# Attention rewritten: layer 0's two attentions in one phase, 256-query jobs, row offsets from four side-by-side products, one maximum over four heads

## The chip, the core and the metric

The kernel runs on one core of a Trainium2 chip. The metric is the device time of one execution in microseconds (us). The engines are TensorE (PE in the profile, its weight loads PEld), VectorE (DVE), ScalarE (ACT), GpSimd (POOL) and SyncE (SP, which here only issues DMAs; SPq is its queue). Each engine runs its own list of instructions in order, and they wait for each other through semaphores.

## What is computed

Two layers, each of an attention block and a mixture of experts, on x of 2 x 1024 tokens, 512 wide, with a context of 2 x 2048 tokens, 256 wide. Only the attention blocks are touched:

```python
# layer 0, 16 heads of 32, on the layer-normed x
att = einsum('bhqd,bhkd->bhqk', q, k) * scale          # 1024 queries x 1024 keys
y = einsum(softmax(where(causal, att, -inf)), v)       # "self", causal
attc = einsum('bhqd,bhkd->bhqk', qc, kc) * scale       # 1024 queries x 2048 keys
y = y + einsum(softmax(attc), vc)                      # "cross"
x = x + tanh(g_xattn[0]) * (y @ Wp + bp)
# layer 1: one cross attention of the same size
x = x + tanh(g_xattn[1]) * (softmax(q1 k1^T * scale) v1 @ Wo + bo)
```

The experts between and behind them, the routing and the projections are the same in both kernels.

## The kernel before

The program is a row of phases: proj0, projc, self0, cross0, out0, route0, ffn0, proj1, attn1, out1, route1, ffn1. A barrier of all engines stands between two phases. A phase of attention works off eight units (2 batches x 4 groups of four heads of 32). The names in the profile are those of the tiles, with digits left out: self_, cross_ and attn_ are the three phases of attention.

A unit is a `Job` with two sides. One is the **scores side**: in steps of 128 keys x 512 queries, PE makes the scores of each of four heads (L692, keys as weights, queries moving), ACT takes their exponentials out of PSUM into `probs` (L789), and PE multiplies these with the values (`pv`) and with ones (`den`), four heads side by side on 32 columns of the array each (L745). About half of the steps leave their sum with ones to POOL, which adds the exponentials up in `psums` (L657), so that `den` takes one product for all of them. A cross unit has 32 such steps, a self unit 12, of which the causal ones are narrower and take a mask product (L696). The other is the **maximum side**: the softmax needs a number to subtract for each query, and it rides in the score product itself. Queries and keys are stored as three stacked blocks of 32 rows (high part, high or low part, low part, so that fp32r products come out exact), and row 96 of the queries holds minus the row's maximum against a row of ones in the keys. These maxima come from a second full score product, with queries as weights and keys moving (L676, mask L680), which VectorE reduces one bank of 512 at a time (L812), or two at a time before the first unit (L823). After the last of a unit, VectorE takes the maximum over the parts, PE transposes it (L721), VectorE negates it (L839), and SP writes it into row 96 by four DMAs (L610).

While one unit's scores side runs, the next unit's maximum side is laid between its products: `timetable` writes one order of events for a pair of units from costs per column, and every engine follows it. The first unit's maxima have nothing to be laid beside: they run alone before the first step of the phase ("group" events), after the loads. Scores go through three banks of PSUM (`BANKS = 3`), and so do the maxima. VectorE inverts the denominators, 512 per partition (L851), and multiplies (L854).

SP loads each unit by eight DMAs (three of keys L586, three of queries L590, two of values L595), three units at the start of a phase, later ones as one of three sets of buffers comes free. The events that the last steps below lean on:

```python
pe.wait_ge(exped, i * (GH * per["steps"]) + (item + 1))   # scores: a bank is free
...
for b in bufs:
    load(next(w for w, j in enumerate(jobs) if j.buf == b), 0, 0)   # SP, at the start
```

## Time and profile before

| | us |
|---|---|
| median of three runs | 4876.4 (4874.72 to 4880.6) |
| span of the profiled execution | 4872.1 |
| self0: first score to the last product of numerator and inverse | 496 to 963 |
| cross0: the same | 1075 to 2056 |
| attn1: the same | 2887 to 3870 |
| PE busy | 4298.1 (88%) |
| VectorE, ScalarE, GpSimd busy | 2731.9, 1960.3, 1360.6 |
| mean granted TensorE clock | 0.903 |

The span is 4.3 us below the median of the runs, and there is nothing of the program outside it. Busy time of PE is the union of its records; a product's record is longer than the distance to the next one, so the distance between starts is what a product costs in a stream. In a view in order of time, a row with a count merges neighbours of one form: its first number is the start of the first, its second the time to the end of the last.

### The profile page before, as it was taken

What the parts mean: (1) busy time and instruction counts of PE and PEld (TensorE: products, weight loads), DVE (VectorE), ACT (ScalarE), POOL (GpSimd) and SP (SyncE); (2) the same over time, 40 slices, a digit from 0 to 9 for tenths busy, and PEclk for the clock granted to TensorE, in tenths of its full rate; (3) what the DMA queues carried; (4) which work ended last, traced back from release to release, by engine and by line L of the source; (5) the groups of instructions that cost most, each with busy time, mean ns of one, the idle gap of its engine ahead of it and who ended that gap; (6) DMA issues with size and microseconds to landing.
All of it is one profiled execution on the core that took longest, in us unless ns stands there. A gap on an engine that the chain in (4) does not pass through costs nothing. (4 is left out here: it accounts for less than half of the span.)

```text
span 4872.1 us, 69058 instructions
## 1 busy us (share of the span) xinstructions
PE 4298.1 (88%) x22146; PEld 2564.5 (53%) x22146; DVE 2731.9 (56%) x4193; ACT 1960.3 (40%) x3433; POOL 1360.6 (28%) x619
## 2 busy tenths in 40 slices
PE   7897999879999999772999489999999763999998
PEld 5776555434444444242998344444444243888886
DVE  4354555367777777147665377767776156434432
ACT  2121333315555555501665215555555401434432
POOL 0000111215555555500111215555555400101111
PEclk9997778859999999975999769999999975999999
DMA  5488233061221220142664552221210032334331
GB/s 170 157 294 246 44 71 70 25 131 23 50 50 41 50 53 5 35 150 77 206 208 151 153 107 47 50 50 42 50 33 5 33 121 97 110 112 122 117 114 37
DMA packets 260270, 451.21 MB, mean 93 GB/s; under 512 B 19216, under 2 KB 102160, under 8 KB 253840
## 3 DMA queue, kind: packets, MB, share of 16 engines
q1 hardware_dynamic: 245904, 409.83, 29.4%
q0 software_dynamic: 14080, 37.76, 3.3%
...
q14 instruction: 130, 1.06, 0.1%
...
## 5 line engine op out<-in xcount | busy, mean ns | idle before, releaser
L657 POOL TENSOR_TENSOR attn_psums<-attn_psums,attn_probs 128x1024 f32<-128x1024 f32 x224 | 531.5, 2396 | 527.4 <-PE attn_pv L745 295.2
L657 POOL TENSOR_TENSOR cross_psums<-cross_psums,cross_probs 128x1024 f32<-128x1024 f32 x224 | 531.4, 2396 | 526.4 <-PE cross_pv L745 294.5
L812 DVE TENSOR_REDUCE attn_partscross<-attn_banks 128x1 f32<-128x512 f32 x896 | 560.1, 683 | 145.9 <-PE attn_banks L676 140.1
L789 ACT ACTIVATE attn_probs<-attn_banks 128x512 f32<-128x512 f32 x960 | 497.9, 604 | 357.6 <-PE attn_banks L692 343.2
L789 ACT ACTIVATE cross_probs<-cross_banks 128x512 f32<-128x512 f32 x960 | 497.8, 604 | 357.3 <-PE cross_banks L692 343.2
L812 DVE TENSOR_REDUCE cross_partscross<-cross_banks 128x1 f32<-128x512 f32 x896 | 560.0, 683 | 145.2 <-PE cross_banks L676 139.8
L676 PE MATMUL cross_banks<-cross_keys,cross_queries 96*128 96x512 f32 x1024 | 408.8, 461 | 37.9 <-DMA cross_values<-l_cross_values 37.9
L676 PE MATMUL attn_banks<-attn_keysy,attn_queriesy 96*128 96x512 f32 x1024 | 408.8, 461 | 37.3 <-DMA attn_valuesy<-l_cross_values 37.3
L1444 DVE TENSOR_TENSOR ffn_wL<-ffn_raw,ffn_wH 128x2048 fp32r<-128x2048 f32 x128 | 293.4, 2293 | 222.6 <-ACT ffn_wH L1399 222.6
L692 PE MATMUL attn_banks<-attn_queriesy,attn_keysy 97*128 97x512 f32 x1024 | 375.3, 425 | 31.1 <-ACT attn_probs L789 19.9
L692 PE MATMUL cross_banks<-cross_queries,cross_keys 97*128 97x512 f32 x1024 | 375.6, 425 | 29.8 <-ACT cross_probs L789 19.7
L1399 ACT ACTIVATE ffn_wH<-ffn_raw 128x2048 fp32r<-128x2048 f32 x128 | 245.2, 1916 | 358.1 <-DMA ffn_raw<-in_L_ffn_W_dram 197.2
L1356 PE MATMUL ffn_up<-ffn_xH,ffn_wH 128*128 128x256 f32 (+1 forms) x1024 | 350.7, 342 | 2.7 <-DVE ffn_xL L1450 2.7
L676 PEld LDWEIGHTS cross_banks<-cross_keys,cross_queries 96*128 96x128 f32 x1024 | 187.9, 204 | 305.9 <-DVE cross_partscross L812 205.4
L676 PEld LDWEIGHTS attn_banks<-attn_keysy,attn_queriesy 96*128 96x128 f32 x1024 | 187.9, 204 | 305.5 <-DVE attn_partscross L812 205.4
L1356 PE MATMUL ffn_up<-ffn_xH,ffn_wL 128*128 128x256 f32 (+1 forms) x1024 | 347.1, 339 | 0.0
L1356 PE MATMUL ffn_up<-ffn_xL,ffn_wH 128*128 128x256 f32 (+1 forms) x1024 | 347.0, 339 | 0.0
L1371 PE MATMUL ffn_down<-ffn_wH,ffn_hH 128*128 128x512 f32 x768 | 306.7, 399 | 0.0
L1371 PE MATMUL ffn_down<-ffn_wH,ffn_hL 128*128 128x512 f32 x768 | 304.5, 396 | 0.0
L1371 PE MATMUL ffn_down<-ffn_wL,ffn_hH 128*128 128x512 f32 x768 | 304.3, 396 | 0.0
L692 PEld LDWEIGHTS attn_banks<-attn_queriesy,attn_keysy 97*128 97x128 f32 x1024 | 187.3, 190 | 209.9 <-ACT attn_probs L789 143.9
L692 PEld LDWEIGHTS cross_banks<-cross_queries,cross_keys 97*128 97x128 f32 x1024 | 187.5, 190 | 209.1 <-ACT cross_probs L789 142.3
...
## 6 DMA issues: line engine op xcount, KB each, us to landing
ffn_raw<-in_L_ffn_W_dram SPq DMA_DIRECT2D x128, 1024.0 KB, 5.4
...
```

Of the source, the lines that this page charges most:

```text
L657: pool.tensor_tensor(psums[:, heads, :], psums[:, heads, :], probs[:, (n["steps"] + s) % RING, heads, :], ALU.add).then_inc(pooled_sum, 1)
L676: mm = pe.matmul(out[:, 0:cols], QS[a.buf][0:3 * HD, h, qt * P:(qt + 1) * P], KS[a.buf][0:3 * HD, h, part * BLK:part * BLK + cols], start= ...
L692: mm = pe.matmul(out[:, n0:], KS[b.buf][0:3 * HD + 1, h, kb * P:(kb + 1) * P], QS[b.buf][0:3 * HD + 1, h, qb * BLK + n0:(qb + 1) * BLK], s ...
L789: act.activation(out[:, h, n0:], sc[:, item % BANKS, n0:], ACT.Exp, scale=SCALE).then_inc(exped, 1)
L812: dve.tensor_reduce(parts[a.kind][:, h * (T // P) + qt, part:part + 1], mx[:, item % BANKS, 0:cols], AX.X, ALU.max).then_inc(max_read, 1)
L1356: mm = pe.matmul(up[ft % UP][:, 0:k], w[:, cols], x[:, ch, :], start=n == 0, stop=n == 3 * C - 1)
L1371: mm = pe.matmul(down[st][:, :], h[:, ft, st * P:(st + 1) * P], w[:, cols], start=ft == 0 and n == 0, stop=ft == FT - 1 and n == 2)
L1399: act.activation(wH[:, m % RING, :], raw[:, m % RING, :], ACT.Copy).then_inc(high_made, 1)
L1444: dve.tensor_tensor(wL[:, m % RING, :], raw[:, m % RING, :], wH[:, m % RING, :].bitcast(F32), ALU.subtract).then_inc(low_made, 1)
```

## The change

`Job` and `timetable` go, and `Unit`, a new `Job` and `Plan` come. A unit is now cut into four jobs of 256 queries, a job into steps of two blocks of 128 keys; a step makes four items of two heads x 256 queries, one bank of PSUM and one exponential each. A cross unit has again 32 steps, a self unit 10. Layer 0's sixteen units (eight self, eight cross) are one phase `attn0` without a barrier between. Nothing is a hardware loop any more.

- The row offset no longer comes from the exact product. The high parts of queries and keys are loaded once more in a flat layout (`QN`, `KN`: head h on partitions 32h to 32h+31), and a group is four products of 32 rows, one per head, into four banks (`mx`, one set for all groups), then four masks where the diagonal is met. VectorE reduces the four banks by one instruction over 4 x 512. PE waits for that before the next group. A job's maxima are due four steps before its first step; 8 groups come before step 0, then mostly one a step in cross units, two in six of the ten steps of a self unit.
- The turned maxima go through a scores bank and are negated by ScalarE; SP writes them by two DMAs per job.
- Numerator and denominator share one bank `acc`; ScalarE takes both out at a job's end. The denominators go by DMA into a layout of 8 per partition, are inverted, go to DRAM and come back spread over 32 partitions; POOL multiplies.
- Two sets of unit buffers in place of three. SP loads unit 0; unit 1 and all later ones are loaded by ScalarE's queue: two flat DMAs right after the unit two back has had its last group, eight stacked ones right after that unit's last step.

The core of the diff:

```diff
+QB = 256
+STEP = 2
+LEAD = 4
...
+class Job:
...
+        if unit.causal:
+            d = 2 * qb
+            self.blocks = [(kb, 0, False) for kb in range(d)] + [(d, 0, True), (d + 1, P, True)]
+        else:
+            self.blocks = [(kb, 0, False) for kb in range(unit.keys // P)]
+        self.steps = len(self.blocks) // STEP
+        self.last = first + self.steps - 1
+        self.groups = []
+        for t in range(QB // P):
+            n = (qb * (QB // P) + t + 1) * P if unit.causal else unit.keys
+            self.parts = -(-n // BLK)
+            for part in range(self.parts):
+                cols = min(BLK, n - part * BLK)
+                self.groups.append((t, part, cols, unit.causal and part == self.parts - 1))
+        whole = [kb for kb, n0, masked in self.blocks if not masked]
+        inner = [kb for kb in whole if kb < len(self.blocks) - 3]
+        self.pooled = [kb for kb in inner if kb < 2 or kb % 2 == 0] if len(inner) > 2 else []
...
+class Plan:
...
+        due = [self.jobs[j].first - LEAD for j, _ in self.groups]
+        done = 0
+        while done < len(due) and due[done] <= 0:
+            self.groups_at[-1].append(done)
+            done += 1
+        for m in range(n):
+            need, k = 0, 0
+            for g in range(done, len(due)):
+                k += 1
+                if due[g] - m > 24:
+                    break
+                need = max(need, -(-k // (due[g] - m + 1)))
+            now = self.jobs[self.job_of[m]]
+            for _ in range(max(need, 1)):
+                if done == len(due):
+                    break
+                j = self.groups[done][0]
+                if j > self.job_of[m] + 3 or self.jobs[j].u > now.u + 1:
+                    break
+                self.groups_at[m].append(done)
+                done += 1
...
+            self.turn_at[m + 2 if m >= 0 and m + 2 < n else -1 if m < 0 else m].append(j)
...
-def attention(nc, name, c, jobs, body, repeats, sources, yT, ring=2):
+def attention(nc, name, c, units):
...
+    RING, SC, DEEP, BUFS = 3, 3, 4, 2
+        KS = [ph.sb(f"keys{b}", [P, GH, KEYS], F32R) for b in range(BUFS)]
+        KN = [ph.sb(f"keysn{b}", [P, KEYS], F32R) for b in range(BUFS)]
+        QN = [ph.sb(f"queriesn{b}", [P, T], F32R) for b in range(BUFS)]
+        sc = ph.ps("sc", (P, SC, BLK))
+        mx = ph.ps("mx", (P, GH, BLK))
+        acc = ph.ps("acc", (P, 2, QB))
...
+        def load_flat(eng, u):
+            unit, b = units[u], u % BUFS
+            eng.dma_start(KN[b][:, 0:unit.keys].bitcast(F32), unit.k_src[unit.row, :, 0, :]).then_inc(flat_in[b], DMA)
+            eng.dma_start(QN[b][:, :].bitcast(F32), unit.q_src[unit.row, :, 0, :]).then_inc(flat_in[b], DMA)
+        def load_stack(eng, u):
+            unit, b = units[u], u % BUFS
+            for row, half in ((0, 0), (1, 1), (2, 0)):
+                eng.dma_start(KS[b][row * HD:(row + 1) * HD, :, 0:unit.keys].bitcast(F32),
+                              unit.k_src[unit.row, :, half, :].rearrange("(h d) n -> d h n", d=HD)
+                              ).then_inc(stack_in[b], DMA)
+            for row, half in ((0, 0), (1, 0), (2, 1)):
+                eng.dma_start(QS[b][row * HD:(row + 1) * HD, :, :].bitcast(F32),
+                              unit.q_src[unit.row, :, half, :].rearrange("(h d) n -> d h n", d=HD)
+                              ).then_inc(stack_in[b], DMA)
...
+                load_flat(sp, 0)
+                load_stack(sp, 0)
+                for j in plan.turn_at[-1]:
+                    set_row(j)
+                for m in range(N_STEPS + 8):
+                    for back, move in ((2, take_den), (3, put_inv), (4, take_over), (7, store)):
+                        if 0 <= m - back < N_STEPS and plan.ends(m - back) is not None:
+                            move(plan.ends(m - back))
+                    for j in plan.turn_at.get(m, ()):
+                        set_row(j)
...
+                def maxima(k):
+                    j, g = plan.groups[k]
+                    job, (t, part, cols, masked) = jobs[j], jobs[j].groups[g]
+                    b = job.u % BUFS
+                    if job.qb == 0 and g == 0:
+                        pe.wait_ge(flat_in[b], FLAT * DMA * (job.u // BUFS + 1))
+                    if k:
+                        pe.wait_ge(max_read, k)
+                    q0 = (job.qb * (QB // P) + t) * P
+                    for h in range(GH):
+                        rows_h = slice(h * HD, (h + 1) * HD)
+                        mm = pe.matmul(mx[:, h, 0:cols], QN[b][rows_h, q0:q0 + P],
+                                       KN[b][rows_h, part * BLK:part * BLK + cols], start=True, stop=True)
+                    if masked:
+                        for h in range(GH):
+                            mm = pe.matmul(mx[:, h, cols - P:cols], c["identr"][:, :], c["maskq"][:, :],
+                                           start=False, stop=True, skip_group_check=True)
+                    mm.then_inc(max_ready, 1)
...
+                def scores(m, i):
+                    j, item = plan.job_of[m], plan.item[m, i]
+                    job = jobs[j]
+                    b = job.u % BUFS
+                    if m == job.first and i == 0:
+                        if job.qb == 0:
+                            pe.wait_ge(stack_in[b], STACK * DMA * (job.u // BUFS + 1))
+                        pe.wait_ge(row_set[j % DEEP], ROW * DMA * (j // DEEP + 1))
+                    if item >= SC:
+                        pe.wait_ge(exped, item - SC + 1)
+                    kb, n0, masked = job.blocks[(m - job.first) * STEP + i // 2]
+                    for half in range(2):
+                        h = 2 * (i % 2) + half
+                        out = sc[:, item % SC, half * QB:(half + 1) * QB]
+                        mm = pe.matmul(out[:, n0:], KS[b][0:3 * HD + 1, h, kb * P:(kb + 1) * P],
+                                       QS[b][0:3 * HD + 1, h, job.qb * QB + n0:(job.qb + 1) * QB], start=True, stop=True)
+                        if masked:
+                            mm = pe.matmul(out[:, n0:n0 + P], c["identr"][:, :], c["maskk"][:, :],
+                                           start=False, stop=True, skip_group_check=True)
+                    mm.then_inc(scored, 1)
...
+                pe.wait_ge(ones_set, BUFS)
+                for k in plan.groups_at[-1]:
+                    maxima(k)
+                for j in plan.turn_at[-1]:
+                    turn(j)
+                for m in range(N_STEPS + 1):
+                    if m < N_STEPS:
+                        for i in range(3):
+                            scores(m, i)
+                        for k in plan.groups_at[m]:
+                            maxima(k)
+                    if m:
+                        values(m - 1)
+                    if m < N_STEPS:
+                        for j in plan.turn_at[m]:
+                            turn(j)
+                        scores(m, 3)
...
+                load_flat(act, 1)
+                load_stack(act, 1)
+                for j in plan.turn_at[-1]:
+                    turned(j)
+                for m in range(N_STEPS + 1):
+                    if m < N_STEPS:
+                        for i in range(3):
+                            exponent(m, i)
+                    if m and plan.ends(m - 1) is not None:
+                        drain(plan.ends(m - 1))
+                    if m < N_STEPS:
+                        for j in plan.turn_at[m]:
+                            turned(j)
+                        exponent(m, 3)
+                    for u in range(len(units) - BUFS):
+                        if m == max(plan.unit_max_at[u], 0) + 1:
+                            act.wait_ge(max_ready, plan.unit_groups[u])
+                            load_flat(act, u + BUFS)
+                        if m == plan.last_of[u] + 1:
+                            act.wait_ge(valued, plan.last_of[u] + 1)
+                            load_stack(act, u + BUFS)
...
+                def reduce(k):
+                    j, g = plan.groups[k]
+                    t, part, cols, _ = jobs[j].groups[g]
+                    dve.wait_ge(max_ready, k + 1)
+                    dve.tensor_reduce(parts[j % DEEP][:, :, t, part], mx[:, :, 0:cols], AX.X, ALU.max
+                                      ).then_inc(max_read, 1)
+                    if g == len(jobs[j].groups) - 1:
+                        dve.wait_ge(max_read, k + 1)
+                        if j >= 2:
+                            dve.wait_ge(exped, plan.turn_item[j - 2] + 1)
+                        dve.tensor_reduce(top[:, j % 2, :].rearrange("p (t h) -> p h t", h=GH),
+                                          parts[j % DEEP][:, :, :, 0:jobs[j].parts], AX.X, ALU.max
+                                          ).then_inc(top_ready, 1)
...
-        for kind, keys_n, own, y in (("self", T, (queries, keys, values), y_self),
-                                     ("cross", TC, (cross_queries, cross_keys, cross_values), y_cross)):
-            jobs = [Job(kind, f"{u % 3}", keys_n, kind == "self") for u in range(UNITS)]
-            attention(nc, f"{kind}0", c, jobs, 3, 2, {kind: own}, y)
+        attention(nc, "attn0", c,
+                  [Unit(T, True, queries, keys, values, y_self, u) for u in range(UNITS)] +
+                  [Unit(TC, False, cross_queries, cross_keys, cross_values, y_cross, u) for u in range(UNITS)])
...
-        jobs = [Job("cross", f"y{u % 3}", TC, False) for u in range(UNITS)]
-        attention(nc, "attn1", c, jobs, 3, 2, {"cross": (l1_queries, l1_keys, l1_values)}, y1)
+        attention(nc, "attn1", c, [Unit(TC, False, l1_queries, l1_keys, l1_values, y1, u) for u in range(UNITS)])
```

The order of PE in the middle of a cross unit, before (cross_banks are scores and maxima, L692 the scores and L676 the maximum products, pv and den values and sums):

```order
L676 MATMUL cross_banks<-cross_keys,cross_queries 128x512 [waits cross0_max_read] x2
L692 MATMUL cross_banks<-cross_queries,cross_keys 128x512 [waits cross0_exped]
L676 MATMUL cross_banks<-cross_keys,cross_queries 128x512 [waits cross0_max_read]
L692 MATMUL cross_banks<-cross_queries,cross_keys 128x512 [waits cross0_exped] x2
L676 MATMUL cross_banks<-cross_keys,cross_queries 128x512 [waits cross0_max_read]
L692 MATMUL cross_banks<-cross_queries,cross_keys 128x512 [waits cross0_exped]
L745 MATMUL cross_pv<-cross_probs,cross_values 32x512 [waits cross0_exped]
L745 MATMUL cross_pv<-cross_probs,cross_values 32x512 x3
L676 MATMUL cross_banks<-cross_keys,cross_queries 128x512 [waits cross0_max_read] x3
L745 MATMUL cross_den<-cross_probs,keep_onesf 32x512 x4
```

One step of a cross unit on PE now, from the last item of the step before on (attn_sc are scores, attn_mx the group of the maximum, attn_acc values and sums):

```order
L682 MATMUL attn_sc<-attn_queries,attn_keys 128x256 [waits attn0_exped]
L682 MATMUL attn_sc<-attn_queries,attn_keys 128x256
L682 MATMUL attn_sc<-attn_queries,attn_keys 128x256 [waits attn0_exped]
L682 MATMUL attn_sc<-attn_queries,attn_keys 128x256
L682 MATMUL attn_sc<-attn_queries,attn_keys 128x256 [waits attn0_exped]
L682 MATMUL attn_sc<-attn_queries,attn_keys 128x256
L682 MATMUL attn_sc<-attn_queries,attn_keys 128x256 [waits attn0_exped]
L682 MATMUL attn_sc<-attn_queries,attn_keys 128x256
L653 MATMUL attn_mx<-attn_keysn,attn_queriesn 128x512 [waits attn0_max_read]
L653 MATMUL attn_mx<-attn_keysn,attn_queriesn 128x512 x3
L699 MATMUL attn_acc<-attn_probs,attn_values 32x256 [waits attn0_exped]
L699 MATMUL attn_acc<-attn_probs,attn_values 32x256 x7
```

Four maximum products scattered among the scores have become one group between the third item's scores and the values, and the first item in the piece is the one whose exponential the fourth item of the piece waits for.

ScalarE at the change of a cross unit now (attn_both is the taking out of numerator and denominator); before, these DMAs stood on SP and ScalarE had none:

```order
L758 ACTIVATE attn_probs<-attn_sc 128x512 [waits attn0_scored] x2
L767 ACTIVATE attn_both<-attn_acc 128x512 [waits attn0_normed,attn0_job_done]
L758 ACTIVATE attn_probs<-attn_sc 128x512 [waits attn0_scored]
L541 DMA attn_keys<-l_cross_keys 32x4x2048 [waits attn0_valued]
L541 DMA attn_keys<-l_cross_keys 32x4x2048 x2
L545 DMA attn_queries<-l_cross_queries 32x4x1024 x3
L550 DMA attn_values<-l_cross_values 128x8x128 x2
L758 ACTIVATE attn_probs<-attn_sc 128x512 [waits attn0_scored,attn0_added,attn0_valued]
```

Eight DMAs now stand between two exponentials.

## Rows read from the trace of the kernel before

**Rows 1.** Busy time by stage, first score to last output (columns: stretch, length, busy by engine with count, granted clock, DMA share, GB/s)
```profile
496.00:963.00 467.00, 451.41 (x2615) 251.50 (x2615) 247.83 (x398) 174.07 (x401) 79.15 (x32) 0.80 0.22 49
1075.00:2056.00 981.00, 950.85 (x5127) 400.58 (x5127) 645.23 (x958) 537.93 (x1040) 531.45 (x224) 0.99 0.16 34
2887.00:3870.00 983.00, 950.71 (x5127) 400.59 (x5127) 645.70 (x958) 539.19 (x1041) 531.46 (x224) 0.99 0.16 34
```

**Rows 2.** PE in order of time, middle of cross0 (start, length, engine, line, tiles, count)
```profile
1501.79 0.40 PE L676 MATMUL cross_banks<-cross_keys,cross_queries 96*128 96x512 f32 x1
1502.03 0.42 PE L692 MATMUL cross_banks<-cross_queries,cross_keys 97*128 97x512 f32 x1
1502.38 1.06 PE L745 MATMUL cross_pv<-cross_probs,cross_values 128*32 128x512 f32 x8
1503.37 0.96 PE L676 MATMUL cross_banks<-cross_keys,cross_queries 96*128 96x512 f32 x3
```

**Rows 3.** Groups by line, shapes kept apart, cross0 (count, busy us, mean ns, idle before)
```profile
L812 DVE TENSOR_REDUCE cross_partscross<-cross_banks 128x1 f32<-128x512 f32 x896 | 560.0, 683 | 145.2 <-PE cross_banks L676 139.8 <-issue 3.6 <-DVE cross_y L854 0.2
L823 DVE TENSOR_REDUCE cross_partscross<-cross_banks 128x2 f32<-128x1024 f32 x64 | 72.5, 1210 | 34.2 <-PE cross_banks L676 34.2
L789 ACT ACTIVATE cross_probs<-cross_banks 128x512 f32<-128x512 f32 x960 | 497.8, 604 | 357.3 <-PE cross_banks L692 343.2 <-POOL cross_psums L657 11.4 <-issue 2.7
L657 POOL TENSOR_TENSOR cross_psums<-cross_psums,cross_probs 128x1024 f32<-128x1024 f32 x224 | 531.4, 2396 | 526.4 <-PE cross_pv L745 294.5 <-ACT cross_probs L789 231.9
```

**Rows 4.** PE in order of time, ffn0: fp32r products of 256 columns
```profile
2402.03 0.28 PE L1356 MATMUL ffn_up<-ffn_xL,ffn_wH 128*128 128x256 f32 x1
2402.15 0.28 PE L1356 MATMUL ffn_up<-ffn_xH,ffn_wL 128*128 128x256 f32 x1
```

**Rows 5.** PE in order of time, self0: 256- and 128-column groups of four heads
```profile
801.22 0.61 PE L745 MATMUL self_den<-self_probs,keep_onesf 128*32 128x256 f32 x8
801.65 1.04 PE L745 MATMUL self_den<-self_psums,keep_onesf 128*32 128x512 f32 x8
...
802.73 0.40 PE L745 MATMUL self_den<-self_probs,keep_onesf 128*32 128x128 f32 x8
803.06 0.50 PE L692 MATMUL self_banks<-self_queries,self_keys 97*128 97x512 f32 x1
803.40 0.22 PE L696 MATMUL self_banks<-keep_maskk,keep_identr 128*128 128x128 f32 x1
```

**Rows 6.** PE in order of time, cross0 after a unit's last maximum
```profile
1188.67 0.94 PE L692 MATMUL cross_banks<-cross_queries,cross_keys 97*128 97x512 f32 x3
1189.84 0.50 PE L692 MATMUL cross_banks<-cross_queries,cross_keys 97*128 97x512 f32 x1 [0.23 <-ACT cross_probs L789]
```

**Rows 7.** SP's queue in order of time: one unit's load, self0 and cross0
```profile
566.77 1.57 SPq L586 DMA_DIRECT2D self_keys<-l_keys  x3
568.43 1.60 SPq L590 DMA_DIRECT2D self_queries<-l_queries  x3
570.22 1.32 SPq L595 DMA_DIRECT2D self_values<-l_values  x2
...
1206.56 1.59 SPq L586 DMA_DIRECT2D cross_keys<-l_cross_keys  x3
1209.99 16.15 SPq L595 DMA_DIRECT2D cross_values<-l_cross_values  x2
```

**Rows 8.** Order of time, all engines: how the three phases begin
```profile
438.75 1.50 SPq L586 DMA_DIRECT2D self_keys<-l_keys  x3
...
962.25 0.69 DVE L854 TENSOR_TENSOR self_y<-self_numer,self_denom 128x512 f32<-128x512 f32 x1
...
1074.78 2.76 PE L692 MATMUL cross_banks<-cross_queries,cross_keys 97*128 97x512 f32 x5 [4.30 <-DMA cross_queries<-cross_topT]
...
2779.43 1.30 SPq L586 DMA_DIRECT2D attn_keysy<-l_cross_keys  x3
...
2887.32 2.27 PE L692 MATMUL attn_banks<-attn_queriesy,attn_keysy 97*128 97x512 f32 x4 [4.36 <-DMA attn_queriesy<-attn_topT]
```

**Rows 9.** Busy time and DMA rate while attn1's first loads run
```profile
2781.00:2802.00 21.00, 0.00 (x0) 0.00 (x0) 0.00 (x0) 0.00 (x0) 18.94 (x3) 0.50 1.01 207
```

602 lines of the change are left out of this document (214 added, 388 removed).

## The prediction

> **What bounds the kernel now.** I read the busy time by stage first. In the two cross stages PE is busy 951 of 981 and 983 us at a granted clock of 0.99, while VectorE has 645, ScalarE 400 to 540 and POOL 531; self0 has PE at 451 of 467 but the clock at 0.80 [rows 1]. So PE's stream is the bound, and I cost it by distances between starts: a 512-column product of scores or maxima 0.24 (1501.79 to 1502.03), one block of values over four heads 0.99 with leaving the column mode, and 0.35 in place of 0.24 before it, so 0.11 for going in [rows 2]; 256 columns 0.12 [rows 4]; four heads of 256 columns 0.43, of 128 columns 0.33 with 0.11 of leaving, and the first product after them 0.34, so 0.10 of weight load that nothing hides [rows 5]. Per cross step of before that gives scores 4 x 0.236 = 0.94, maxima the same, values 0.86, sums 9/16 x 0.86 = 0.48, and 1.56 visits to the column mode x 0.3 = 0.47: 3.70, against 981/256 = 3.83 measured. The account misses 3 to 4% of small waits; I carry that on.
>
> **Part 1, a cross step (512 of them).** The maxima shrink from four exact products to one group. No row of before shows four products of 32 rows side by side. If they run like the column groups, a group costs one product, 0.24, plus 0.10 for its weights and 0.09 for the change of mode: 0.43. If they run one by one, it costs 0.94 + 0.1 = 1.04. I take the lower end less a little of the weight load, 0.41, since the nearest rows are the column groups: four heads leave eight records there, which one by one at 0.24 would need 1.9 and take 0.88 [rows 2], so they do lie side by side.
> The gain is not the whole 0.6, because of the scores' ring. There are three banks as before, but the order is now fixed: item 3 of a step, items 0, 1 of the next, and item 2 waits until item 3's exponential is out. The trace shows that chain by itself: three scores from 1188.67, the next at 1189.84, released by ScalarE, 1.17 later [rows 6], where three items need only 0.72. Two products of 256 end together as one of 512 does (0.12 + 0.28 is near 0.42 to 0.50 [rows 2, 4, 6]). So a step is: chain 1.17, item 2 with exposed weights 0.34, group 0.41, into the column mode 0.09, values 2 x 0.44 = 0.88, sums 18/16 x 0.43 = 0.48, out 0.11: 3.48. The turns of the maxima add 0.06, unmodelled waits 0.05: **3.6**. A phase's eight units give 256 x 3.6 = 922, plus 10 for the last job's denominators (three DMA hops, of which one shows as 4.3 [rows 8]): 932 against 981 and 983. **-100** for both.
> What hides the rest: VectorE's reduce of 4 x 512. Its slope is (1210 - 683)/512 = 1.03 ns a column [rows 3], so 683 + 3 x 512 x 1.03 = 2265 ns; with the group ahead of it and the semaphores its cycle is 2.84 of 3.6, and PE's wait for the previous reduce costs nothing. That cover is 0.75 us; below a step of 2.85 VectorE would set the pace. ScalarE has 4 x 0.60, POOL seven sums of 2.4 per eight steps [rows 3]: neither binds. ScalarE's taking out of a job's bank, one more instruction of about 0.6 per eight steps, and the row writes, 4.3 us a hop [rows 8] against a lead of four steps (14 us), I cost at nothing: next late would be PE's first values of a job, a step behind the taking out.
>
> **Part 2, the loads on ScalarE.** Before, SP issues a unit's eight DMAs and nobody waits for SP. A cross unit's take it from 1206.56 to 1226.14, 19.6 us, of which 16.15 are the two of values, against 4.8 us for a self unit (566.77 to 571.54) [rows 7]. SP is thus held until much of what is queued has moved. Now the same eight stand in ScalarE's queue between two exponentials. PE can run on until it needs an exponential, about 1.4 us; then it stands. I take 19.6 - 1.4 + 2 (PE comes back at the granted 0.50 that an idle PE has [rows 9]; estimate) = 20 us. Fourteen stack loads are of cross size (units 8 to 15 of attn0, six in attn1): **+280**. The two bounds of the price: 16.15 is a queue's hold that ScalarE may not have, then 5 us as for self (14 x 17.5 = 245 less); at the rate of 207 GB/s [rows 9] the stack's 5.8 MB take 28 us, if the issue were held to the end: 14 x 8 = 112 more. The row of the very same eight transfers is nearest. The flat loads, two DMAs of about 0.5 each, hide under PE's lead. The Trainium skill's page "DMA: Bandwidth & Descriptors", section "Issuing engines are not separate DMA queues", says that the sequencer time of initiating is usually small relative to the transfer; by that rule these +280 would be about +35, and the row of 16.15 us speaks against it here.
>
> **Part 3, the self stage.** Before, 467/8 = 58.4 per unit [rows 1]. Now a unit has 10 steps of 20 blocks and 12 groups. PE's work: scores and masks 13.1 (10.5 at full clock, divided by the 0.80 of the stage), groups 12 x 0.41 = 4.9, their masks 3.5, values 16 x 0.43 + 4 x 0.22 = 7.8, sums 5.6, changes of mode 2.0: 36.9. Waits: the ring 10 x 0.4 = 4.0; the second group of a step waits for the reduce of the first, six times, 0.68 + 1.74 + 4 x 2.26 + 6 x 0.23 = 12.9; turns 0.8; the self-size stack load 4.8 - 1.6 = 3.2. That is 57.8; two more because the clock, at 0.80 with PE nearly full, will hardly rise with PE two thirds full: 60, **+14** over eight units. Here the saved products are paid back as waits for one set of `mx`.
>
> **Part 4, ends of phases.** The barrier and the cold start of cross0 go: from 962.25 + 0.69 to 1074.78 [rows 8]: **-112**. That stretch held loads and the first unit's maxima alone; the maxima of unit 8 now fall into the last self unit's free steps, its loads are in flight a unit earlier. The starts that stay: attn0 loads two units at once, 9.4 MB at 207 GB/s [rows 9] = 46 us from 438.75 [rows 8], first score at 486 against 496: **-10**. attn1: 14.7 MB, 71 us from 2779.43, first score 2852 against 2887.32 [rows 8]: **-36**; its eight groups (26 us) hide under the rest of that load.
>
> **Sum:** -100 + 280 + 14 - 112 - 10 - 36 = +36 on 4872.1. The profiled span lies 4.3 below the median of the runs: 4876.4 + 36 = 4912; I say 4910.
>
> **The rivals.**
> *A, the queue does not hold ScalarE.* Its ring has no other traffic, while SP's carried row writes and outputs; then a stack load costs 4 to 5 us of issue as self's does: 4910 - 245 = 4665, faster than before. For it: six of the eight issues are short even in the cross row. Against: the two long ones are the last, which looks like a full queue and not like SP. It decides from about 17 us a load downwards: under 20 - 36/14 = 17.4 the sum is below zero.
> *B, the four products do not run side by side.* Then a group costs 0.60 more: 512 x 0.60 = 307, about 5215. The change would not do what it says. Against it: column groups do run so [rows 2, 5]. The Trainium skill ("TensorE: Matmul & The Clock Gate", Part 3) has four row tiles of 32 with N = 512 measured at 3.07 times one by one; 0.94/3.07 = 0.31 would be the group, 0.1 under mine; that lowers B's chance, and no row here bears on it.
> *C, the ring does not bite.* If item 3's exponential comes sooner than the case of [rows 6] tells, where ScalarE may have been behind, the step is 3.2: 512 x 0.4 = 205 less, 4705. Against: 1.17 is product, 0.60 exponential and semaphores, all still there.
> *D, the self stage gets a worse clock.* PE busy 37 of 60 may hold the granted clock nearer to the 0.50 of an idle PE [rows 9] than to 0.80; 36.9 x (0.80/0.62 - 1) = 10 per unit: +80, 4990. For it: the clock is at 0.80 already with more work [rows 1].
>
> **How the numbers follow.** Forecast 0.43 (own range 4800 to 5010: the step +-0.1 gives +-50, the load +-3 us gives +-42, the self stage +-20), A 0.16, B 0.09, C 0.14, D 0.18. About +-0.2%, 10 us, is what a measurement of this kernel can tell from no change. Faster: A, C and a fifth of the forecast's case, 0.39; same: a sixth of that case, 0.07; slower: its rest, B and D, 0.54. The range holds 8 in 10 from 4640 (just under A) to 5130 (D or the forecast with the longer hold; most of B, and A with C, lie outside).
>
> **What would show it.** On ScalarE at each change of a cross unit a stretch of some 16 to 20 us without an exponential, PE idle beside it, 14 times; cross steps at 3.6 with item 2's first product idle about 0.4 behind ScalarE, once a step; a group's four products starting within 0.1 of each other (B: 0.24 apart); VectorE's reduce near 2.26 us; the second group of a self step waiting for VectorE; self units near 60 and the granted clock there 0.75 to 0.80 (D: under 0.7); first scores near 486 and, in attn1, some 71 us behind its first load. The forecast is wrong above all if a load holds ScalarE for much less or more than 20 us, since that term alone decides the sign.

## The result

The changed kernel takes 4926.6 us (median of 4 runs, 4925.3 to 4927.5) against 4875.6 of the kernel before (4 runs): a ratio of 1.0105, 95% interval 1.0091 to 1.0119, 51 us slower. Forecast were 4910 and +36. The profiled execution spans 4925.9 us, 53.8 more than before's.

The busy time by stage of the changed kernel, with the columns of [rows 1] (the last three are granted clock, DMA share and GB/s). The five stretches are the start of attn0 up to the first score, its self units, its cross units, the start of attn1, and attn1:

```profile
438.00:481.00 43.00, 12.30 (x59) 8.10 (x59) 12.99 (x11) 0.48 (x2) 13.77 (x2) 0.50 0.98 220
481.00:1045.00 564.00, 450.49 (x3754) 300.33 (x3754) 190.93 (x160) 184.63 (x382) 115.33 (x70) 0.70 0.34 82
1045.00:2093.00 1048.00, 871.92 (x9502) 515.41 (x9500) 572.62 (x310) 554.72 (x1089) 555.76 (x258) 0.93 0.25 58
2817.00:2882.00 65.00, 7.08 (x34) 2.76 (x35) 18.53 (x9) 1.55 (x2) 13.78 (x2) 0.50 0.99 226
2882.00:3923.00 1041.00, 874.15 (x9471) 516.11 (x9470) 578.71 (x311) 553.45 (x1087) 554.24 (x256) 0.93 0.22 52
```

Against [rows 1]: PE is busy 872 and 874 us in place of 951 in each cross stage, and yet the stages are 58 to 67 us longer. The self stage has the same busy time, 450 against 451, in 97 us more, and its granted clock is 0.70, not 0.80.

The table sets what each term was forecast to bring beside what the two traces show. A unit's length is the distance between its first score and the next unit's.

| term | forecast | measured | from |
|---|---|---|---|
| cross steps, 512 | -100 | -118 | 8 units of 1048 and 1041 us less their load stalls (7 and 6 of 18.7), against 981 and 983 |
| 14 cross stack loads on ScalarE | +280 | +255 | a cross unit with a load is 132.5 in the mean of 13, and 113.9 if its first three steps are as long as without one (4.36, 3.14 and 3.49): 18.7 x 13, and 12 in the last self unit (PE's wait of 9.5 there, the rest an estimate for its return at the lower clock) |
| self stage without that one | +14 | +85 | 564 - 12 against 467 |
| gap between self and cross | -112 | -112 | not there |
| starts of attn0 and attn1 | -46 | -58 | from the first load to the first score 43.1 against 57.5, and 64.5 against 107.9 |
| all other phases | 0 | +1 | what is left of 53.8 |
| sum | +36 | +54 | of unrounded terms |

PE in a cross unit of the changed kernel, in order of time (start, length, line, tiles, count), answering [rows 2, 6]:

```profile
1500.45 0.50 PE L682 MATMUL attn_sc<-attn_queries,attn_keys 97*128 97x256 f32 x2 [0.21 <-ACT attn_probs L758]
1500.88 0.50 PE L653 MATMUL attn_mx<-attn_keysn,attn_queriesn 32*128 32x512 f32 x4
1501.32 1.07 PE L699 MATMUL attn_acc<-attn_probs,attn_values 128*32 128x256 f32 x16
1502.20 0.61 PE L706 MATMUL attn_acc<-attn_probs,keep_onesf 128*32 128x256 f32 x8
1502.75 0.98 PE L682 MATMUL attn_sc<-attn_queries,attn_keys 97*128 97x256 f32 x6
1503.94 0.50 PE L682 MATMUL attn_sc<-attn_queries,attn_keys 97*128 97x256 f32 x2 [0.21 <-ACT attn_probs L758]
```

The step is 1503.94 - 1500.45 = 3.49 us. The group of four products takes 0.44 to the first product of values (1500.88 to 1501.32), at 0.41 and the way into the column mode as costed; the four start within 0.01 us of each other, so they do lie side by side. The chain of the scores' ring is 1503.94 - 1502.75 = 1.19 (forecast 1.17). The idle time shown is only 0.21, because the record of the product ahead of it runs on; by starts the wait is 0.47. This account of a cross step held. One thing it had not: the first three steps of attn1 hold two groups each and take 6.1, 8.3 and 8.1 us, so that unit is 11 us longer than one without a load; this lies in the -118.

ScalarE and its queue, where unit 10 begins. The row of the exponential behind the DMAs has its idle time in brackets:

```profile
1315.36 0.59 ACT L758 ACTIVATE attn_probs<-attn_sc 128x512 f32<-128x512 f32 x1
1315.64 1.24 ACTq L541 DMA_DIRECT2D attn_keys<-l_cross_keys  x2
1316.91 1.45 ACTq L545 DMA_DIRECT2D attn_queries<-l_cross_queries  x3
1318.40 14.56 ACTq L550 DMA_DIRECT2D attn_values<-l_cross_values  x2
1333.08 1.08 ACT L758 ACTIVATE attn_probs<-attn_sc 128x512 f32<-128x512 f32 x2 [17.13 <-issue]
```

And PE beside it, which comes back 15.78 us later:

```profile
1316.88 1.07 PE L699 MATMUL attn_acc<-attn_probs,attn_values 128*32 128x256 f32 x16
1333.73 0.58 PE L682 MATMUL attn_sc<-attn_queries,attn_keys 97*128 97x256 f32 x1 [15.78 <-ACT attn_probs L758]
```

The issue of the values is held for 14.56 us as on SP before (16.15, [rows 7]), and ScalarE is now the engine held. The rule of the Trainium skill weighed in the prediction ("DMA: Bandwidth & Descriptors", "Issuing engines are not separate DMA queues") doesn't describe this load: 18.7 us of a unit went with its issue.

The same hold stands in the start of attn1. PE has turned the first unit's last maximum at 2856.88, but ScalarE, which has to take it out, has been issuing unit 1's load since 2817 and is held at its values for 43.83 us, while SP's two value DMAs for unit 0, issued at the same moment, take 3.08:

```profile
2821.89 43.83 ACTq L550 DMA_DIRECT2D attn_values<-l_cross_values  x2
2865.77 0.27 ACT L746 ACTIVATE attn_topT<-attn_sc 8x128 fp32r<-8x128 f32 x1 [54.94 <-issue]
2881.70 1.62 PE L682 MATMUL attn_sc<-attn_queries,attn_keys 97*128 97x256 f32 x6 [24.45 <-DMA attn_queries<-attn_topT]
```

The bytes of the two loads move for just as long (226 GB/s up to 2882, 2 GB/s in the 8 us behind), so this trace doesn't part the hold from the transfer.

The self stage, one step with two groups, PE:

```profile
805.51 0.51 PE L653 MATMUL attn_mx<-attn_keysn,attn_queriesn 32*128 32x512 f32 x4
808.41 0.48 PE L653 MATMUL attn_mx<-attn_keysn,attn_queriesn 32*128 32x128 f32 x4 [2.40 <-DVE attn_parts L797]
808.82 1.11 PE L657 MATMUL attn_mx<-keep_maskq,keep_identr 128*128 128x128 f32 x4
809.87 1.51 PE L699 MATMUL attn_acc<-attn_probs,attn_values 128*32 128x256 f32 x16
811.15 1.51 PE L706 MATMUL attn_acc<-attn_probs,keep_onesf 128*32 128x256 f32 x16
```

PE waits 2.40 us for VectorE's reduce between the groups, as costed (2.26 and the way to and fro; VectorE's row has 2293 ns, x560). The values behind it take 811.15 - 809.87 = 1.28 us where the same sixteen records took 0.88 in the cross step above. That is the second loss, and the one that the sum had almost left out: these products run at a granted clock of 0.50, the cross step above at 1.00.

### The profile page after: what moved, and what is told of

It is laid out like the page before. It is cut to its first block and busy times, and to the rows that moved or that the text cites. A ratio compares the mean times of both kernels' runs of the same rounds, so it can differ in the third digit from the quotient of the medians.

```text
span 4925.9 us, 78762 instructions
## 1 busy us (share of the span) xinstructions
PE 3994.9 (81%) x31754; PEld 2769.2 (56%) x31754; DVE 2396.8 (49%) x2500; ACT 2001.3 (41%) x3511; POOL 1414.5 (29%) x718
## 5 line engine op out<-in xcount | busy, mean ns | idle before, releaser
L797 DVE TENSOR_REDUCE attn_parts<-attn_mx 128x4 f32<-128x2048 f32 (+2 forms) x608 | 1343.0, 2209 | 1196.2 <-PE attn_mx L653 1044.9
L758 ACT ACTIVATE attn_probs<-attn_sc 128x512 f32<-128x512 f32 (+1 forms) x2368 | 1218.8, 597 | 985.4 <-PE attn_sc L682 623.4
L682 PE MATMUL attn_sc<-attn_queries,attn_keys 97*128 97x256 f32 (+1 forms) x4736 | 940.7, 320 | 359.2 <-ACT attn_probs L758 323.5
L637 POOL TENSOR_TENSOR attn_psums<-attn_psums,attn_probs 128x1024 f32<-128x1024 f32 x408 | 969.3, 2376 | 475.3 <-ACT attn_probs L758 448.9
L682 PEld LDWEIGHTS attn_sc<-attn_queries,attn_keys 97*128 97x128 f32 x4736 | 695.1, 200 | 694.1 <-ACT attn_probs L758 467.3
L699 PE MATMUL attn_acc<-attn_probs,attn_values 128*32 128x256 f32 (+1 forms) x9472 | 676.7, 407 | 1.4 <-ACT attn_probs L758 1.4
L634 POOL TENSOR_TENSOR attn_psums<-attn_probs 128x1024 f32<-128x1024 f32 x80 | 189.8, 2373 | 1005.3 <-ACT attn_probs L758 1005.3
L653 PE MATMUL attn_mx<-attn_keysn,attn_queriesn 32*128 32x512 f32 (+3 forms) x2432 | 322.2, 518 | 173.3 <-DVE attn_parts L797 133.7
L699 PEld LDWEIGHTS attn_acc<-attn_probs,attn_values 128*32 128x32 f32 x9472 | 258.5, 114 | 258.9 <-issue 147.8
L706 PE MATMUL attn_acc<-attn_probs,keep_onesf 128*32 128x256 f32 x4928 | 385.1, 404 | 0.0
```

What stands on the lines that cost most here:

```text
L634: pool.tensor_tensor(ps, probs[:, m % RING, 0, :, :], at, ALU.add).then_inc(added, 1)
L637: pool.tensor_tensor(ps, ps, at, ALU.add).then_inc(added, 1)
L653: mm = pe.matmul(mx[:, h, 0:cols], QN[b][rows_h, q0:q0 + P], KN[b][rows_h, part * BLK:part * BLK + cols], start=True, stop=True)
L682: mm = pe.matmul(out[:, n0:], KS[b][0:3 * HD + 1, h, kb * P:(kb + 1) * P], QS[b][0:3 * HD + 1, h, job.qb * QB + n0:(job.qb + 1) * QB], sta ...
L699: mm = pe.matmul(acc[h * HD:(h + 1) * HD, 0, n0:], VS[b][:, kb, h * HD:(h + 1) * HD], probs[:, m % RING, i, h, n0:], start=kb == 0, stop=k ...
L706: mm = pe.matmul(acc[h * HD:(h + 1) * HD, 1, n0:], c["onesf"][:, 0:HD], probs[:, m % RING, i, h, n0:], start=False, stop=False, skip_group ...
```

## Experiments

All edits are made on the changed kernel (4926.6 us); a difference below is to that time where nothing else is said.

### The loads on SyncE

The lines stand in SyncE's loop over the steps, and the same lines are gone from ScalarE:

```diff
                    for j in plan.turn_at.get(m, ()):
                        set_row(j)
+                    for u in range(len(units) - BUFS):
+                        if m == max(plan.unit_max_at[u], 0) + 1:
+                            sp.wait_ge(max_ready, plan.unit_groups[u])
+                            load_flat(sp, u + BUFS)
+                        if m == plan.last_of[u] + 1:
+                            sp.wait_ge(valued, plan.last_of[u] + 1)
+                            load_stack(sp, u + BUFS)
```

> All loads after unit 1 stand in SyncE's queue in place of ScalarE's, behind the same waits; everything else is the changed kernel (4926.6 us). Theory, the loads hold ScalarE and PE with it: the 14 stretches of 17 to 19 us without an exponential are gone, a cross unit falls from 132.5 to 114.5 us (32 steps of 3.57), self units lose 1 to 2 us each: 14 x 18 + 10 = 260 less, about 4665. Rival, what matters is the transfer and not who issues it (a first step of the unit waits for its data, or the row writes stand behind the load on SyncE and PE waits for a row): the stall moves to PE's wait for attn_queries and the time stays within 50 us of 4927.

Measured 5043.1 us, 117 slower. ScalarE has no exponential behind an issue any more, but PE now waits for VectorE at the maxima. The waits of PE added up (total, times, longest), SP's queue, VectorE and PE in order of time at one change of unit:

```profile
PE attn_mx L660 <- DVE attn_parts L797: 472.0, 78, 22.8
```

```profile
1361.03 16.59 SPq L550 DMA_DIRECT2D attn_values<-l_cross_values  x2
1377.66 4.51 SPq L571 DMA_DIRECT2D attn_den<-attn_both  x1
```

```profile
1386.09 0.20 DVE L812 RECIPROCAL attn_inv<-attn_den 128x8 f32<-128x8 f32 x1 [23.25 <-DMA attn_den<-attn_both]
```

```profile
1388.51 0.80 PE L660 MATMUL attn_mx<-attn_keysn,attn_queriesn 32*128 32x512 f32 x4 [21.89 <-DVE attn_parts L797]
```

The load holds SP; the denominators' DMA stands behind it; VectorE, in order, stands at the inverse; PE stands at the next group, for which VectorE must have read the banks. Theory and rival both named the wrong place. What it costs to hold a queue's owner depends on the small transfers that share the queue.

### The same, behind the denominators

```diff
-                        if m == plan.last_of[u] + 1:
+                        if m == plan.last_of[u] + 5:
```

> As the first experiment (e1_sp, all later loads on SyncE), but the stack load stands four steps later, behind the job's denominators instead of ahead of them. Theory, e1_sp was slow because SyncE, held by the load, issued the denominators' DMA 20 us late, VectorE stood at the inverse behind it, and PE at the maxima behind VectorE (472 us): with the denominators ahead of the load that chain is gone and nothing replaces ScalarE's stall: about 4665, at most 4700. Rival, a load on SyncE delays something else as long (the store, the next row): 4900 or more.

Measured 4887.0 us: 40 faster than the changed kernel and 156 faster than the first try, so the chain through VectorE is real. But the rival was right in kind: at the next job's first step PE waits for the row, 166 us in 13 waits where the changed kernel has 26 in 4. SP's queue, and PE:

```profile
1194.27 15.05 SPq L550 DMA_DIRECT2D attn_values<-l_cross_values  x2
1209.37 6.86 SPq L588 DMA_DIRECT2D l_y_cross<-attn_y  x1
1216.33 1.23 SPq L564 DMA_DIRECT2D attn_queries<-attn_topT  x2
```

```profile
1220.01 1.65 PE L689 MATMUL attn_sc<-attn_queries,attn_keys 97*128 97x256 f32 x6 [12.74 <-DMA attn_queries<-attn_topT]
```

### Values first

```diff
         def load_stack(eng, u):
             unit, b = units[u], u % BUFS
+            t = unit.keys // P // 2
+            for half in range(2):
+                eng.dma_start(VS[b][:, half * t:(half + 1) * t, :],
...
             for row, half in ((0, 0), (1, 1), (2, 0)):
...
             for row, half in ((0, 0), (1, 0), (2, 1)):
...
-            t = unit.keys // P // 2
-            for half in range(2):
-                eng.dma_start(VS[b][:, half * t:(half + 1) * t, :],
...
```

> The two value DMAs stand first among the eight of a stack load, still in ScalarE's queue. Theory, the issue is held because the queue is full, not because value transfers are slow to issue: the long issue moves to the last DMAs, the queries, and the sum stays 17 to 20 us, the time within 30 us of 4927. Rival, the value DMAs (many short rows) are slow to issue by themselves: their issue stays at 15 us as first ones.

Measured 4838.0 us, 89 faster, and neither reading held. ScalarE and its queue, at a change of unit:

```profile
1308.28 0.39 ACTq L542 DMA_DIRECT2D attn_values<-l_cross_values  x1
1308.70 0.60 ACTq L542 DMA_DIRECT2D attn_values<-l_cross_values  x1
1309.33 2.00 ACTq L546 DMA_DIRECT2D attn_keys<-l_cross_keys  x3
1311.36 1.42 ACTq L550 DMA_DIRECT2D attn_queries<-l_cross_queries  x3
1312.90 3.63 ACT L758 ACTIVATE attn_probs<-attn_sc 128x512 f32<-128x512 f32 x7 [3.95 <-issue]
```

The values are issued in 1.0 us when nothing is ahead of them, and the hold doesn't pass to the queries, though the bytes are the same: a load holds ScalarE 4 us in place of 17. But the unit falls only from 132.5 to 125.0 us. The 13 us less of hold come back in part at the next job's first step, where PE now waits for the row: 4.27 us at 1215.96, and 27 us in all in attn0's cross stage, against 1.4 in the changed kernel. The step ahead of it takes 6.5 to 8.6 us in place of 3.5. So the order of the eight decides how long their issue is held. It is not value DMAs alone that can be held: at the start of attn1 in the kernel before, the first key DMA of the second unit, right behind two of values, takes 7.07 us to issue (2797.03). Why this order is not held (rows in DRAM are 512 bytes for values, 8 and 4 KB for keys and queries) no run here settles.

### One DMA per step

`load_stack(act, u, i)` issues the i-th of the eight alone:

```diff
-                        if m == plan.last_of[u] + 1:
-                            act.wait_ge(valued, plan.last_of[u] + 1)
-                            load_stack(act, u + BUFS)
+                        i = m - plan.last_of[u] - 1
+                        if i == 0:
+                            act.wait_ge(valued, plan.last_of[u] + 1)
+                        if 0 <= i < STACK:
+                            load_stack(act, u + BUFS, i)
```

> The eight stack DMAs of a load are issued by ScalarE one per step over eight steps, in place of all at once. Theory, the hold comes from what is queued at once: one DMA per step (at most 1 MB per 3.5 us against 207 GB/s, so it is gone by the next) is issued in 0.5 us and no exponential comes late: 14 x 18 + 6 x 2 = 260 less, about 4665. Rival, each value DMA holds the queue for its own transfer, 5 us: a hold of two times 3 to 4 us per load stays, about 4750.

Measured 4768.5 us, 158 faster. The hold is gone: ScalarE's waits for issues beside exponentials come to 0.2 us in all, and each DMA is issued in 0.3 to 0.4 us, the values too:

```profile
1195.91 0.40 ACTq L553 DMA_DIRECT2D attn_values<-l_cross_values  x1
```

The theory was right in kind and 100 us too hopeful. A cross unit with a load falls from 132.5 to between 119 and 124 us, not to 114: some 6 us remain. In those units the fourth step is 7 to 8 us long, where VectorE waits for the denominators, and the eighth, behind which PE waits for the next job's row, is mostly 1 to 2 us longer than the others. The self units didn't gain (71.7 each): their loads had not been their trouble.

### Two groups apart

```diff
-                        for k in plan.groups_at[m]:
+                        for k in plan.groups_at[m][:1]:
                            maxima(k)
                    if m:
                        values(m - 1)
+                    if m < N_STEPS:
+                        for k in plan.groups_at[m][1:]:
+                            maxima(k)
```

> Where a step has two or more groups of the maximum, all but the first are issued by PE behind the values and sums, not back to back. Theory, self units take 70.5 us in place of 58.4 because PE stands 2.4 us for VectorE between two groups and then works on at the half clock: the wait hides under the values and sums (2 to 2.6 us), the clock comes back, a self unit falls to 55 to 60 us: 85 to 120 us less in all, 4805 to 4840. Rival, the self stage is long by its products and masks alone (narrow ones, changes of mode): at most the six waits of 2.4 us less what VectorE still asks, under 40 us less, 4890 or more.

Measured 4803.1 us, 123 faster, just beyond the theory's range, and all of it in the self stage, which falls from 564 to 439 us at a granted clock of 0.84:

```profile
483.00:922.00 439.00, 372.40 (x3752) 250.86 (x3753) 189.88 (x160) 182.57 (x382) 115.59 (x70) 0.84 0.43 105
```

The same steps on PE, a wait of 0.5 us in place of 2.4 and the values of a partly narrow step in 0.68 us (752.36 to 753.04), which take 1.29 in the same step of another unit in the changed kernel (762.55 to 763.84):

```profile
751.93 0.51 PE L653 MATMUL attn_mx<-attn_keysn,attn_queriesn 32*128 32x512 f32 x4
752.36 0.86 PE L699 MATMUL attn_acc<-attn_probs,attn_values 128*32 128x256 f32 x16
753.04 0.83 PE L706 MATMUL attn_acc<-attn_probs,keep_onesf 128*32 128x256 f32 x16
...
754.83 0.45 PE L653 MATMUL attn_mx<-attn_keysn,attn_queriesn 32*128 32x384 f32 x4 [0.53 <-DVE attn_parts L800]
```

### A shorter reduce in self units

```diff
-                    dve.tensor_reduce(parts[j % DEEP][:, :, t, part], mx[:, :, 0:cols], AX.X, ALU.max
+                    seen = min(cols, P) if jobs[j].unit.causal else cols
+                    dve.tensor_reduce(parts[j % DEEP][:, :, t, part], mx[:, :, 0:seen], AX.X, ALU.max
```

> In causal units VectorE reduces only the first 128 columns of each bank, so that part of the maximum is left out there; PE's stream is unchanged, only its wait between two groups is shorter (0.7 in place of up to 2.3 us). Theory, waits lower the granted clock and the clock costs more than the waits: the waits shrink by 6 to 8 us a unit, and the clock rises from 0.71 to 0.8 or more, which gives 4 to 6 us more: self units 56 to 60 us in place of 70.5, about 90 to 110 us less in all. Rival, the clock doesn't hang on these waits: 6 to 8 us a unit and no more, the granted clock stays at 0.71, 50 to 60 us less.

Measured 4843.7 us, 83 faster. PE's stream is untouched here, so this run parts the wait from the clock. The self stage and PE's waits in it, then the same waits of the changed kernel:

```profile
483.00:955.00 472.00, 404.24 (x3755) 269.29 (x3756) 95.54 (x160) 181.43 (x382) 115.49 (x70) 0.79 0.41 98
```

```profile
PE attn_mx L653 <- DVE attn_parts L798: 46.5, 47, 2.4
```

```profile
PE attn_mx L653 <- DVE attn_parts L797: 97.6, 47, 2.4
```

The stage loses 92 us. Half of it, 46, is idle time (these waits fall by 51, others grow by 5), and half is the same products at a granted clock of 0.79 in place of 0.70: PE's busy time falls from 450 to 404 us. Here a wait saved brought nearly its own length a second time, in the clock of the work around it. The theory holds, if a little below its size. Busy time times granted clock (0.704 and 0.787 unrounded) is 317 us in the changed kernel and 318 here, so the fall of busy time is the clock's.

### The group ahead of the third item

```diff
-                        for i in range(3):
+                        for i in range(2):
                             scores(m, i)
                         for k in plan.groups_at[m]:
                             maxima(k)
+                        scores(m, 2)
```

> The group of the maximum stands ahead of the third item's scores in place of behind them. Theory, the step of 3.49 us contains a wait for the ring of three score banks (1.19 us from an item's score to the release of its bank, where the three scores between are 0.72): the group of 0.43 fills it, the step falls by 0.47 less one more exposed weight load and change of mode (0.1 to 0.2): 0.3 x 512 = 150 us less, about 4775. Rival, the gap of 0.21 shown as idle is all there is to win and the extra changes of mode eat it: within 30 us of 4927.

Measured 4799.5 us, 127 faster. An ordinary step falls from 3.49 to 3.21 us; the ring's wait is filled by the group (PE, in order of time):

```profile
1504.55 0.98 PE L682 MATMUL attn_sc<-attn_queries,attn_keys 97*128 97x256 f32 x6
1505.46 0.51 PE L653 MATMUL attn_mx<-attn_keysn,attn_queriesn 32*128 32x512 f32 x4
1505.90 0.51 PE L682 MATMUL attn_sc<-attn_queries,attn_keys 97*128 97x256 f32 x2
```

So the wait of 0.47 was there, and the 0.2 that did not come back fit the exposed weights and change of mode of the theory, which no row parts. The two cross stages are 50 and 52 us shorter, less than 0.28 in each of 256 steps would give, since the stall of a load grew by some 2 us. The other 25 us fall in the self stage: its waits for VectorE are as before (97.9 us), yet the granted clock there is 0.74 in place of 0.70 and PE's busy time 427 in place of 450. So the clock doesn't follow from the sum of these waits alone.

### Two phases again

```diff
-        attention(nc, "attn0", c,
-                  [Unit(T, True, queries, keys, values, y_self, u) for u in range(UNITS)] +
-                  [Unit(TC, False, cross_queries, cross_keys, cross_values, y_cross, u) for u in range(UNITS)])
+        attention(nc, "self0", c,
+                  [Unit(T, True, queries, keys, values, y_self, u) for u in range(UNITS)])
+        attention(nc, "cross0", c,
+                  [Unit(TC, False, cross_queries, cross_keys, cross_values, y_cross, u) for u in range(UNITS)])
```

> The self units and the cross units of layer 0 are two phases again, with the barrier between, all else as in the changed kernel (4926.6 us). Theory, joining them is worth the start of a cross phase (64 us from the first load to the first score, as in layer 1, and 14 us of a phase's end) less two stack loads of cross size that no longer hold ScalarE (2 x 18) and less the cross groups in the last self unit (10 us): 30 to 45 us more, about 4965. Rival, the joining is worth the full 112 us that the gap took before: about 5040.

Measured 4958.4 us, 32 slower, as the theory had it: joining the phases is worth 32 us in the new form of the kernel and not the 112 of the old gap. In the new form a cross phase starts 68 us after the self phase (the last self output at 1007.9, the first cross score at 1076.0), where [rows 8] have 112. The other 44 us belong to the new start, not to the joining: cheaper maxima, and two units loaded by two queues where one loaded three. No run parts these. The maxima no longer end the start: ScalarE and SP are held by the two loads until 1058.9 and 1059.8, and only then is the turned one taken out and its row written. Against the gap of 68 us, the self stage is 39 us shorter than in the changed kernel (525 against 564: the last unit holds neither the cross unit's load nor its maxima, and the drain behind it is counted in) and the cross stage 6 us shorter. What is left, some 8 us, is spread over other stages and the distance of the profiled runs from the medians.

### Three edits together, and three more tries

e7_spread, e2_late and e3_early in one kernel:

> Three edits together on the changed kernel: the stack DMAs one per step (e7_spread alone: -158 us), further groups of a step behind the values (e2_late: -123), the first group ahead of the third item's scores (e3_early: -127). Theory, the three act on different waits (ScalarE's queue, VectorE in self units, the score ring in cross steps) and add up except for the part of e3_early that shortened self units: 4926 - 158 - 123 - 127 + 20 = 4540. Rival, with the shorter step another engine's cycle (VectorE 2.8, ScalarE 2.4 plus its issue) or the small transfers behind a load (row writes, denominators) binds: 4600 or more.

Measured 4512.4 us, ratio to the kernel before 0.9251, interval 0.9236 to 0.9267: 414 us faster than the changed kernel, where the three alone gave 158 + 123 + 127 = 408. The three gains add up to within 6 us; the overlap of 20 that the theory took off did not show. The self stage and the cross stage of attn0:

```profile
483.80:890.00 406.20, 364.13 (x3755) 245.38 (x3755) 190.90 (x160) 186.29 (x382) 115.91 (x70) 0.88 0.45 113
890.00:1793.00 903.00, 859.42 (x9427) 512.62 (x9425) 570.99 (x308) 554.37 (x1083) 553.45 (x257) 0.97 0.28 67
```

What a load still costs was the next question. First, more slack for VectorE's inverse:

```diff
-                    if 0 <= m - 2 < N_STEPS and plan.ends(m - 2) is not None:
-                        invert(plan.ends(m - 2))
+                    if 0 <= m - 3 < N_STEPS and plan.ends(m - 3) is not None:
+                        invert(plan.ends(m - 3))
```

SP's steps for the inverses, the spread and the store, and POOL's product, move one step later with it.

> As e11_three, and VectorE's inverse of a job stands one step later in its queue (with the steps that follow from it). Theory, in e7_spread a cross unit takes 120 us and not 114 because the denominators' small DMA lies behind the load's large ones and VectorE, in order, holds up the maxima: one more step of slack takes away 3 of the 6 us per unit: 14 x 3 = 40 us less than e11_three. Rival, the rest is the row writes, which this doesn't move: within 10 us of e11_three.

Measured 4525.8 us, 13 slower. The wait went from one place to another: PE's waits for VectorE fell from 119.8 to 77.1 us, and those for the row writes rose from 47.9 to 105.9. SP's queue shows why:

```profile
1123.20 0.34 SPq L577 DMA_DIRECT2D attn_rows<-attn_inv  x1
1134.32 2.82 SPq L583 DMA_DIRECT2D attn_over<-attn_rows  x4
1137.24 1.22 SPq L565 DMA_DIRECT2D attn_queries<-attn_topT  x2
```

The inverses, 4 KB, take 11 us to land while a load is in flight (1.4 us elsewhere). SP waits for that landing, and the next job's row stands behind it; moved one step later, it came nearer to that row.

Then the starts: unit 1's stack also one DMA per step, and PE waits for POOL's ones behind the first maxima and not ahead of them.

```diff
-                load_stack(act, 1)
...
+                    if m < STACK:
+                        load_stack(act, 1, m)
```

> As e12_later, and unit 1's stack DMAs at the start of a phase are also issued one per step, beside unit 0's steps, and PE waits for the ones of POOL only before the first scores. Theory, the first score waits for two units' loads where one is needed: attn1's first score comes 25 to 30 us sooner, attn0's 5 to 8 us (eight groups with one mx set take the rest): 30 to 35 us less than e12_later. Rival, the maxima alone set the start: under 10 us.

Measured 4501.4 us, ratio 0.9232, interval 0.9215 to 0.9249, the fastest of all: 24 less than e12_later. The first score of attn0 comes 8 us sooner but its first unit is 5 us longer; attn1's comes 40.3 us behind its first load in place of 64.7, so unit 1's load had set it (its bytes and ScalarE's hold together) and not the maxima alone. Last, a thinner load (unit 1's of attn1 too), without e12_later's edit:

```diff
+                        apart = 3 if not units[u + 1].causal else 1
-                        if 0 <= i < STACK:
-                            load_stack(act, u + BUFS, i)
+                        if 0 <= i < STACK * apart and i % apart == 0:
+                            load_stack(act, u + BUFS, i // apart)
```

> As e13_start, without the later inverse of e12_later, and beside cross units the stack DMAs are issued in every third step in place of every one. Theory, what is left of a load's price (a cross unit takes 113 to 117 us, 103 to 106 without any wait) is that small transfers (denominators, inverses, row writes) take 5 to 11 us behind 5.8 MB moved at full rate, in place of 1.4 to 2, and VectorE, SyncE or PE stand for them: at a third of the rate the waits go, 5 to 7 us a unit: 4501 - 14 for the later inverse taken back - 14 x 6 = 4400. Rival, small transfers are late behind any single 1 MB DMA: the waits are spread and not shortened, 4480 or more.

Measured 4563.0 us, 62 slower than e13_start; the rival was right. The two edits are not parted by a run of their own, but e12_later's alone had cost 13 us, so taking it back does not explain the loss. Cross units with a load take 118 to 123 us in place of 114 to 117: the fourth step is again 8 to 9 us long, as in e11_three, and the eighth and ninth take 7 to 8, where e11_three has 4.5 to 5.4 and 4.2 to 5.9. SP's queue behind a single key DMA, issued by ScalarE at 1117.57:

```profile
1117.78 0.58 SPq L572 DMA_DIRECT2D attn_den<-attn_both  x1
1125.29 0.34 SPq L577 DMA_DIRECT2D attn_rows<-attn_inv  x1
```

With one DMA of 1 MB ahead of them the denominators take 7.3 us from issue to VectorE's inverse (1125.06), against 1.9 at the end of the phase in the changed kernel, and spread over 24 steps the load meets three jobs' small transfers instead of one's.

## Why the prediction was right, step by step

**The bound and the cross step** were right: -118 against -100, the step 3.49 (3.56 with turns and ends of jobs) against 3.48 (3.6). Both doubtful rows were read rightly: the group costs 0.44 with its entry, so rival B fell, and the ring's chain is 1.19, so rival C fell; e3_early took that wait away and the step fell by 0.28. By the Trainium skill (the page "TensorE: Matmul & The Clock Gate", Part 3, 3.07 times) the products alone would take 0.31, an estimate; the trace shows 0.44 with weights and the change of mode, and no row parts them.

**The loads** were right in mechanism and sign and 25 us too dear: 18.7 a unit and not 20. Rival A fell: ScalarE is held as SP was. But the hold hid a second cost, which the prediction had set to nothing: small transfers late behind the load. They come to light when the hold goes: in e7_spread, which has none, some 6 us a unit remain, in e6_vfirst, with 4 us of hold, 11. So e7_spread gained 158 and e6_vfirst 89, not 250. The row writes were costed at nothing under a lead of four steps; that held in attn0's cross units only with ScalarE's stall in the way (1.4 us of waits), and no longer without it (27 us in e6_vfirst, 11.5 in e7_spread).

**The self stage is the step that failed**: +85 against +14. Its waits for VectorE were counted rightly: PE waited 97.6 us in 47 waits over eight units, 12.2 a unit, forecast 12.9. Its own loads were priced too high: 3.2 a unit, where PE waits for ScalarE 2.2 us in all eight besides the cross-size load. The products were too cheap, by two faults. The first is in the sum: only the scores and masks, 10.5 at full clock, are divided by the stage's clock of 0.80; groups, their masks, values, sums and changes of mode, 23.8 us, stand at full clock. Divided too, they are 29.8, so 6 a unit were missing at the forecast's own clock. The second is the clock: 34.3 us of products at full clock are 42.9 at 0.80 and 49.0 at the measured 0.70, another 6, for which the sum had two. These 10 us a unit, an estimate, less the 4 that waits and loads came out under the forecast, leave some 3 of the 9 measured without a name. Rival D had the mechanism and nearly the clock (0.70 against its "under 0.7") and was given 0.18; its +80 is near the 71 over the forecast, in part by luck, since it scaled a sum that was too small by a clock, 0.62, that was too low. e4_short shows the clock's part with the products unchanged.

So the forecast's case and much of D came true together, and the total was near because the loads, the cross steps and the starts were 25, 18 and 12 us better than forecast. The sum is right partly by luck: errors of 71 and 55 us with opposite signs.

**The ends of phases** were right in size: -112 for the gap, -58 against -46 for the starts. The start of attn1 was costed as the transfer of two units at 207 GB/s, 71 us; they moved at 226, which gives 65 for the 64.5 measured. And the gap's 112 is not the worth of joining the phases: e5_apart gives that as 32.

## What to carry over

An engine that issues DMAs can be held with them, and what stands behind the issue decides the price. Moving the load from ScalarE to SyncE cost 117 us; issuing it in pieces between the steps gained 158. A stall that goes may show the next one behind it, so price a change by the whole unit and not by the wait. Before giving successive groups of products one set of PSUM banks, look for places where two follow back to back: here the wait was paid once as idle time and nearly once more in the granted clock. When a stage's clock is below 1, divide all its products by it, not some. And put work of PE between an item and the one that waits for its bank: here a change of order alone gave 127 us, and with the two other edits turned a kernel 1% slower into one 7.5% faster than before.

## What the runs showed of the chip

- Two value DMAs are issued in 0.4 to 0.6 us each when nothing is ahead of them or they stand alone in a step, and are held 14.6 us behind six DMAs of keys and queries. With the values first, the keys and queries behind them take 0.5 to 0.7 us each. Key DMAs can be held too: 7.07 us behind two value DMAs at the start of attn1 in the kernel before. With two units loaded at once by two queues, ScalarE's value DMAs were held 43.83 us and SP's 3.08 (attn1 of the changed kernel), or both, 43 and 45 us (cross0 of e5_apart). The cause stays open.
- The denominators, 4 KB on SP's queue, 1.9 us otherwise, take 7.3 us behind one DMA of 1 MB issued by ScalarE; the inverses, 4 KB, 1.4 us otherwise, take 11 us during a load.
- With the same products, the self stage's PE busy time went 450, 427, 404 and 372 us at granted clocks of 0.70, 0.74, 0.79 and 0.84 (after, e3_early, e4_short, e2_late); busy time times clock is 313 to 318 in all four, from the unrounded clocks. PE's waits for VectorE were 97.6, 97.9, 46.5 and 49.3 us: fewer waits went with a higher clock, but e3_early against the changed kernel and e2_late against e4_short differ in clock with nearly the same sum of waits. What beside the waits decides is open.
